# Four-layer image kernel: y of two directions in one accumulator, the next direction's operands made one image early, and a free order of the units

## What is computed

```python
def step(h, inp):
    dt_t, B_t, C_t, u_t = inp
    dA = jnp.exp(dt_t[..., None] * A)
    h = dA * h + (dt_t * u_t)[..., None] * B_t[:, None, :]
    y = jnp.einsum('bdn,bn->bd', h, C_t)
    return (h, y)
...
y = ys.transpose(1, 0, 2) + uc * Dp
y = y * jax.nn.silu(z)
return jnp.einsum('bld,od->blo', y, out_proj_w)
```

## Time and profile before

| | us |
|---|---|
| median of three executions | 13798.05 |
| the profiled execution | 13793.3 |
| its span, first to last instruction | 13791.5 |
| PE busy | 12088.6 (88%) |
| DVE busy | 12598.5 (91%) |
| ACT busy | 12052.7 (87%) |
| POOL busy | 12608.1 (91%) |

### The profile page before, as it was taken

The page is one execution under the profiler, slowest core; times in us unless marked ns, Lnnn a source line. Parts: engine busy times, 40 slices in busy tenths (PEclk is TensorE's granted clock), DMA queues, the critical chain, the costliest instruction groups (busy, mean ns, idle before and its releaser), DMA issues.

```text
span 13791.5 us, 184501 instructions
## 1 busy us (share of the span) xinstructions
PE 12088.6 (88%) x68188; PEld 8349.2 (61%) x68188; DVE 12598.5 (91%) x8502; ACT 12052.7 (87%) x18757; POOL 12608.1 (91%) x3786
## 2 busy tenths in 40 slices
PE   7888889898888888888888888888888888888886
PEld 4566666666666666666666666666666666666654
DVE  7999999999999999999999999999999999999985
ACT  6889888889888898888898888888888988889875
POOL 6999999999999999999999999999999999999985
PEclk8999999999999999999999999999999999999987
DMA  5555555555555555555555555555555555555552
GB/s 188 217 222 218 220 213 223 224 213 221 221 217 219 219 217 222 218 219 221 215 222 217 221 220 220 218 216 222 218 223 215 219 217 218 224 215 222 217 200 110
DMA packets 517060, 2965.20 MB, mean 215 GB/s; under 512 B 57818, under 2 KB 57914, under 8 KB 253890
## 3 DMA queue, kind: packets, MB, share of 16 engines
q1 hardware_dynamic: 516162, 2953.40, 56.8%
HBM read 2889.73 MB, written 46.66 MB: 213 GB/s over the span
## 4 chain that ended last, share of the span: by engine, by line
POOL 27%; issue 25%; DVE 18%; ACT 16%; PE 12%; DMA 0%; POOLq 0%; DVEq 0%; SPq 0%; ACTq 0%
POOL ring L983 18%; DVE ring L1469 10%; POOL ring L966 8%; DVE slot L1455 6%; PE work L1481 5%; PE y_acc L1496 4%; ACT L1000 4%; ACT ring L1160 3%; ACT z_t L1069 2%; PE slot L1496 2%; ACT slot L1160 2%; PE y_acc L1481 1%; ACT work L1052 1%; ACT stack L1050 1%; DVE du L1282 1%
## 5 line engine op out<-in xcount | busy, mean ns | idle before, releaser
L983 POOL TENSOR_TENSOR ring<-ring,c_rows 128x2048 f32<-128x2048 f32 x2048 | 9295.3, 4546 | 814.1 <-DVE ring L1469 809.7
L1469 DVE TENSOR_TENSOR_SCAN ring<-ring,slot 128x1024 f32<-128x1024 f32 x2752 | 6251.9, 2281 | 161.9 <-ACT ring L1160 66.4
L1496 PE MATMUL y_acc<-wk,ring 128*128 128x128 f32 x32768 | 4506.5, 285 | 625.6 <-POOL ring L983 592.6
L1496 PEld LDWEIGHTS y_acc<-wk,ring 128*128 128x128 f32 x32768 | 3975.3, 147 | 1431.0 <-POOL ring L983 766.2
L966 POOL TENSOR_TENSOR ring<-du,b_rows 128x1024 f32<-128x1024 f32 x1344 | 3182.1, 2369 | 180.9 <-PE y_acc L1496 77.4
L1469 DVE TENSOR_TENSOR_SCAN ring<-slot,ring 128x1024 f32<-128x1024 f32 x1344 | 3058.3, 2276 | 277.3 <-POOL ring L966 244.6
L1160 ACT ACTIVATE ring<-dt,a_neg 128x1024 f32<-128x1024 f32 x2752 | 3069.7, 1140 | 52.0 <-PE y_acc L1496 42.2
L1455 DVE TENSOR_TENSOR slot<-du,slot 128x1024 f32<-128x1024 f32 x1952 | 2361.8, 1210 | 53.1 <-PE slot L1481 50.0
L1000 ACT ACT_TABLE_LOAD x1825 | 2341.5, 1283 | 32.0
L1069 ACT ACTIVATE z_t<-du_t,b_t 128x128 f32<-128x128 f32 x6400 | 2037.1, 391 | 40.1 <-PE slot L1496 17.5
L1481 PE MATMUL work<-h_new,fused 128*128 128x512 f32 x4096 | 1914.3, 601 | 46.1 <-ACT b_t L1072 30.6
(11 more groups left out here) (178 smaller groups left out, 9800.0 us busy)
## 6 DMA issues: line engine op xcount, KB each, us to landing
c_rows<-cb_rows_scratch SPq DMA_DIRECT2D x2048, 1024.0 KB, 4.6
b_rows<-cb_rows_scratch SPq DMA_DIRECT2D x1344, 512.0 KB, 5.5
x_next<-in_x SPq DMA_DIRECT2D x32, 512.0 KB, 5.6
x_new_scratch<-x_next SPq DMA_DIRECT2D x32, 512.0 KB, 6.7
h_old<-h_new SPq DMA_DIRECT2D x32, 512.0 KB, 3.2
x_old<-x_new_scratch SPq DMA_DIRECT2D x32, 512.0 KB, 7.3
out<-x_old SPq DMA_DIRECT2D x32, 512.0 KB, 3.2
cb_rows_scratch<-stack SPq DMA_DIRECT2D x128, 100.0 KB
```

Of the source, the lines that this page charges most:

```text
L983: pool.tensor_tensor(pair, pair, c_rows[:, k % CB_BUFS, :, :], ALU.mult).then_inc(prod_ready, 1)
L1469: dve.tensor_tensor_scan(slot, a, b, 0.0, MUL, ADD).then_inc(scan_done, 1)
L1496: ins = pe.matmul(chunk(out_t, j), chunk(x, j), kc("ident"), is_transpose=True, start=start and j % (BANK // P) == 0, stop=stop, skip_grou ...
```

## The change

**Order of the units.** `pass_of` and `parts_of` put the half outside and the direction inside within each pair of directions. The passes of an image run (d, h) = (0,0), (1,0), (0,1), (1,1), (2,0), (3,0), (2,1), (3,1).

**Accumulator.** `y_acc` is started with every 32nd unit. Two passes, the two directions of a pair on one half, go into it. The takes on ACT (L1076) and the addition of `yz` in PE (n = 5) are gone. DVE takes after passes 1, 3, 5 and 7, as many as before.

**Operands.** Those of direction 1 (convolution, projection, `cb_rows`) and the first z gate are made in the image in front, behind those of direction 0. For image 0, `begin_plan` makes them. `stack` and `b_t` get a third buffer. SP stores direction 1's rows at the start of an image, and stores those of 2 and 3 ahead of passes 4 and 5.

**Free order.** The units of an engine are lines of their own for the planner: on DVE the D inputs and the scans, on POOL the P inputs and the products, on PE the spreads or turns and the sums. They are laid beside the side steps by due time and readiness. `SHIFTS` has new values, now for units too.

**Kinds.** `KINDS` is new: 53 D, 49 P and 26 Z for an image. By pass, in the new order, P has 6, 6, 7, 6, 7, 6, 5 and 6 (before: 5, 6, 4, 7, 8, 3, 3 and 5).

```diff
-KINDS = ('DPDPDDDDDPZPDPDZ', 'DPDZDPDZDPZPDPDP', 'DDDDDPZPDZDPZDDP', 'DPDPDPZZZPZPDPDP',
-         'DPZPDPZPDPPDZPDP', 'DPDPDPDDDDZZDPDZ', 'DPDPDPDDZZDDDZDZ', 'DPDPDPDDDDZDZPZP')
+KINDS = ('DPPZZDDDZPZPPPDZ', 'DDDDDPZPDPZPPDDP', 'DPDZPDDZPPZPDDPP', 'DZPDDZPZPPZZDPDP',
+         'DPZPPDPZDPPDZDPD', 'DPDPDZPZPDPDDZDP', 'DDPDDPPPDDZDZDPD', 'DPDDZDDDPPDPZPPZ')
...
+    return {"D": [[("b", u) for u in of("D")], [("scan", u) for u in range(UNITS)]],
+            "G": [[("input", u) for u in of("P")], [("prod", u) for u in range(1, UNITS, 2)]],
+            "P": [[("zturn" if kind_of(u) == "Z" else "spread", u) for u in turned], [("sum", u) for u in range(UNITS)]],
+            "A": [[("decay", u) for u in range(UNITS)]]}
...
+        ops += held_back(conv_after(0, 0), ("h1", 1)) + conv_after(1, 0) + conv_after(0, 1) + project_after(0, over(3))
+        ops += gate_z(0, 0, [("take", 5)]) + conv_after(1, 1)
+        ops += rows_after(project_after(1, over(6)), 1, ("scan", UNITS - 5))
...
+    o = held_back(o, ("fuse", 1, TAPS - 1)) + gate_z(0, 0) + conv(1, 0) + conv(1, 1)
+    o += project(1)
...
+                store_rows(1, base, ("A", 0))
...
-                    if n == 5 and d % 2:
-                        halves(y_acc, kc("ident"), yz[:, d // 2, h, :], False, False)
                     pe.wait_ge(prod_ready, s * PAIRS + u // 2 + 1)
-                    turn(y_acc, ring[:, u % RING, :], n == 0, n == NST - 1).then_inc(sum_done, 1)
+                    turn(y_acc, ring[:, u % RING, :], u % (2 * NST) == 0, (u + 1) % (2 * NST) == 0).then_inc(sum_done, 1)
```

More of the change, by code:

```diff
@@ L144, in silu_pair, with conv, gate_z, project @@
     return steps + [step(("silu", of, d, h, c), "A", key(c)) for c in range(2)]
-def operands(d, first=False):
-    steps = []
[L150 to L155, removed]
+def conv(d, h):
+    return silu_pair("u", d, h, "conv_in", [(k,) for k in range(TAPS)])
+def gate_z(f, h, after=()):
+    return silu_pair("z", f, h, "z", [()], after)
+def project(d):
+    steps = []
     for c in range(2):
@@ L456, in wanted @@
             by[("zmul", u, 1)] = u - 1.5
-    by[("take", "before")] = 4
-    for p in range(PASSES - 1):
+    for p in range(1, PASSES - 1, 2):
         by[("take", p)] = p * NST + NST + 4
-    by[("turned_y", "this", 1, 0, 1)] = UNITS - 4
+    by[("silu", "z", 0, 0, 1)], by[("silu", "z", 1, 1, 1)] = UNITS + 2 * NST, UNITS
     want = deadlines(streams, by, pace)
@@ L602, in image_streams @@
     takes = []
-    for p in range(PASSES - 1):
-        f, t, h = p // 4, p // 2 % 2, p % 2
-        after = [("sum", p * NST + NST - 1)]
-        if t == 0 and not first:
-            after += [(("post", 1) if h else ("angles",)) if f else ("mix", 4, 1)]
-        takes += [step(("take", p), "D" if t else "A", None, after)]
-        if t:
-            takes += turn_y("this", f, h)
+    for p in range(1, PASSES - 1, 2):
+        f, h = p // 4, p // 2 % 2
+        after = [("sum", p * NST + NST - 1)] + ([("silu", "z", f, h, 1)] if p > 1 else [])
+        if not first:
+            after += [("angles",) if f else ("mix", 4, 1)]
+        takes += [step(("take", p), "D", None, after)] + turn_y("this", f, h)
     zs = []
@@ L635, in count @@
     def count(steps, e):
-        return sum(x[2] == e for x in steps)
+        return sum(x[1] == e and x[3] is not None for x in steps)
     def bases(kind, s):
@@ L647, in numbers @@
         n, out = dict.fromkeys("PADG", 0), {}
-        for x in steps:
-            n[x[2]] += 1
-            out[x[1]] = (x[2], n[x[2]])
+        for name, e, _, after in steps:
+            if after is not None:
+                n[e] += 1
+                out[name] = (e, n[e])
         return out
@@ L654, in four_layers, with order_of, image_of @@
     plan_n = {kind: numbers(plan) for kind, plan in plans.items()}
-    def at_place(plan, e):
-        out = {}
-        for x in plan:
-            if x[2] == e:
-                out.setdefault(x[0], []).append(x)
-        return out
+    def order_of(plan, e):
+        return [x for x in plan if x[1] == e]
+    def image_of(name, s):
+        k = name[0]
+        if name in front_names or k in ("cb_rows", "part", "rest", "xproj", "turn_b", "turned_b", "conv_in") and name[1] < 2:
+            return s + 1
+        if k == "silu" and name[1] == "u" and name[2] < 2:
+            return s + 1
+        if (k[:3] == "dt_" or k in ("turn_du", "turned_du")) and name[1:3] == (0, 0):
+            return s + 1
+        return s
+    front_names = {x[0] for x in front()}
     with ExitStack() as ctx:
@@ L943, in step @@
                 ins.then_inc(side["G"], 1)
-            for _, name, e, _, after in before:
+            for name, e, _, after in before:
                 if e == "G":
@@ L950, in image @@
             def image(kind, s):
[L951 to L956 removed]
+                base, of = bases(kind, s), plan_n[kind]
                 def make_input(u):
@@ L983, in image @@
                     pool.tensor_tensor(pair, pair, c_rows[:, k % CB_BUFS, :, :], ALU.mult).then_inc(prod_ready, 1)
-                side_steps(END["G"])
+                for name, _, _, after in order_of(plans[kind], "G"):
+                    if name[0] == "input":
+                        make_input(name[1])
+                    elif name[0] == "prod":
+                        times_c(name[1])
+                    else:
+                        hold(pool, "G", base, of, after)
+                        step(name, s)
             each_image(pool, image)
-            for _, name, e, _, after in finish:
+            for name, e, _, after in finish:
                 if e == "G":
@@ L1123, in step @@
                 ins.then_inc(side["A"], 1)
-            for _, name, e, bank, after in before:
+            for name, e, bank, after in before:
                 if e == "A":
@@ L1469, in image @@
                     dve.tensor_tensor_scan(slot, a, b, 0.0, MUL, ADD).then_inc(scan_done, 1)
-                side_steps(END["D"])
+                for name, _, bank, after in order_of(plans[kind], "D"):
+                    if name[0] == "b":
+                        times_b(name[1])
+                    elif name[0] == "scan":
+                        scan(name[1])
+                    else:
+                        hold(dve, "D", base, of, after)
+                        step(name, image_of(name, s), bank_of[bank])
             each_image(dve, image)
-            for _, name, e, bank, after in finish:
+            for name, e, bank, after in finish:
                 if e == "D":
```

365 lines of the change are left out of this document (171 added, 194 removed), and 98 rows, old and new, of the table SHIFTS.

## The result

The changed kernel takes 14372.49 us (median of four, 14369.08 to 14382.40), the kernel before 13797.58 in the same comparison. The ratio is 1.0418, 95% interval 1.0400 to 1.0436: 575 us slower, where 168 us faster was forecast. The profiled execution spans 14367.3 us.

A forecast was written before the change was run, and what follows sets the result against it. DVE was taken to bound some passes and POOL others. Start 130.4, first image 420, thirty middle images 12486, last 450 and finish 138.4 sum to 13624.8, with profile and median offsets 13630 us; range 13440 to 13890.

The forecast's parts named there:

- The store of rows: Direction 1's operands, made one image early: ACT's `cb_rows` should find SP's store done, since it is issued in 0.27 us.
- POOL's waits for scans: Middle images: POOL's 24.0 us an image of waiting for DVE's scans go nearly all.
- the idle term: POOL's idle time in a middle image: 6 us, bounds 0 and 28.5, giving 416.2 us an image.
- its line between faster and slower: POOL's idle time per middle image from which the idle-time rival decides: 11.6 us.
- a balance of loads by pass: All eight passes now ask more of POOL than of DVE, so POOL's waits for scans go nearly all.
- The turn of the image: Between images, direction 1's early operands on ACT: 2 us taken; as slower rival 8 us a turn, 13880 us, chance 0.14.
- POOL's and DVE's work: Middle image, from the new kinds: POOL busy 410.2 us instead of 393.9, DVE 382.8 instead of 392.7.
- The takes: Four ACT copies an image go, 4.1 us of ACT; fewer handovers worth 0 to 2.5 us, counted within the idle time.
- The start: Ahead of the first product: direction 1's operands and z gate add 29 us, between 20 and 40.
- DMA: 7 more B rows of 512 KB, 4% more at a share of 58%, cost nothing.
- POOL's idle time stays: Slower rival: the 28.5 us an image are what engines in fixed order lose to each other; 14350 us, chance 0.11.
- POOL idle over 12 us with DVE full in the same pass: Sign, per image, that would make the forecast wrong.

The follow-up runs named there:

- e1_rows32: The changed kernel with all 32 rows of B and C stored instead of 31; 13969.49 us, ratio 1.0125 to the kernel before.
- e16_pool_load_moved: The kernel before plus four unused POOL products an image at units 91, 93, 97 and 109, away from `group_rstd`; 13854.49 us, ratio 1.0042.
- e14_pool_load: The kernel before plus four unused POOL products an image at units 87, 89, 103 and 107; 14155.19 us, ratio 1.0258.
- e15_act_tie: The kernel before with ACT's decays of units 87, 89, 103 and 107 held for the scan two units back; 13976.34 us, ratio 1.0134.
- e3_in_order: The changed kernel, 31 rows, with each engine's units in the old fixed order and side steps laid anew; 15017.89 us, ratio 1.0885.
- e8_before_no_copy: The kernel before without ACT's four takes an image, PE's waits for them and PE's additions of `yz`; 13818.52 us, ratio 1.0016.
- e17_before_46p_moved: The kernel before with four D units made P at units 92, 94, 98 and 108, away from `group_rstd`; 14248.52 us, ratio 1.0327.

## Why the prediction was wrong, point by point

**The store of rows** is the step that failed first, and the larger part: 13.5 of the 24.4 us by which a middle image missed (440.6 against 416.2). I wrote that such a store is issued in 0.27 us and that ACT "should find the store done". The row prices the issue; what waits is the landing. SP waited 9.7 us a store for it. The row to read stood beside it in the same timeline: the next load 3.0 us after the store, for a store of 25 rows. And the store is not the same after the change, since a line outside the diff derives its row count from `KINDS`. I priced the B rows that are read back and never asked what the new table does to the store.

**POOL's waits for scans** are nearly all of the rest. "The 24.0 us an image that POOL waits for scans go nearly all" was the step on which the forecast rested. With the store mended, 375.8 / 30 = 12.5 us of them stay. The other two waits, put at 4.1 us, measured (70.3 + 65.0) / 30 = 4.5. So the idle term is 17.3 us instead of 6, and the 11.3 us more, with POOL's busy time 0.4 under the forecast, are the rest of the miss. The forecast's own arithmetic holds with it: its line between faster and slower stood at 11.6 us, and 30 x (17.3 - 11.6) = 171 us over 13798 gives 13969, against 13969.5 measured for `e1_rows32`.

The reason I gave was a balance of loads by pass. The traces say where it held. Cut at the first product of each pass, mean of the thirty middle images, POOL's idle time is 4.6, 0.0, 3.9, 5.7, 0.0, 4.2, 3.8 and 6.3 us in the passes 0 to 7 before, and 1.5, 0.0, 0.9, 6.8, 1.7, 0.0, 1.9 and 4.5 in `e1_rows32`. In six passes together it fell from 16.5 us to 6.0, as I had reckoned for all eight. In passes 3 and 7 it stayed: 12.0 before, 11.3 after. There no engine is busy for more than 93% of the pass in either kernel, so a better balance had little to give; the earlier trace rows showed this of pass 3 already. It is also not true that all eight passes now ask more of POOL than of DVE: pass 3 has one P unit less than before, and DVE is busy 57.2 us in it, POOL 56.9. In image 9, pass 7 before; then passes 3 and 7 of `e1_rows32`, and POOL's longest stop in pass 3:

```profile
4267.15:4321.81 54.66, 47.03 (x257) 32.83 (x255) 46.48 (x28) 46.84 (x76) 47.69 (x14) 0.91 0.57 217
```

```profile
4139.62:4203.17 63.55, 53.02 (x285) 34.36 (x285) 57.13 (x44) 58.87 (x104) 56.92 (x21) 0.97 0.52 195
4353.29:4409.81 56.52, 44.25 (x276) 31.63 (x277) 45.96 (x27) 51.27 (x73) 52.30 (x17) 0.97 0.65 246
...
4162.72 4.55 POOL L1049 TENSOR_TENSOR ring<-ring,c_rows 128x2048 f32<-128x2048 f32 x1 [6.15 <-DVE ring L1526]
```

That one stop, in front of the product of units 52 and 53, is 6.2 us in the mean image, half of the 12.5; DVE has layer 2's side steps between the scans there. Whether the six passes gained by the kinds or by the new order was not taken apart. `e16_pool_load_moved` shows that idle time can take load, 7.7 us of 9.5; `e14_pool_load` and `e15_act_tie` show what the balance leaves out, waits that one engine passes on to another. Which ties hold the rest in the new plan is not settled. The waits that grew most are DVE's for slots from PE (50.0 us before, 529.7 after, 363.6 in `e1_rows32`) and ACT's for slots from DVE (270.8, 591.4, 583.3); no run took one of them away alone.

**The turn of the image** was put at 2 us with 8 as its bound. ACT waited 4.5 us there, but for the store (1.3 for PE), and that wait is gone with 32 rows. There POOL idles 2.6 us in front of an image's first product, 2.5 before. As a rival (13880) it did not happen.

**POOL's and DVE's work** came as forecast: POOL 409.8 us an image (410.2), DVE 11513.9 / 30 = 383.8 (382.8). **ACT** has 381.2 instead of 375.4. The new plan changes its function tables more often: 1941 loads at 1.28 us against 1825 before is 116 more, 4.7 us an image. I had no term for it. The free order is not the main reason: `e3_in_order` has 1910.

**The takes** and the handovers were worth nothing (`e8_before_no_copy`, 24 us slower), just under the low end of what I gave them. **The start** grew by 34.9 us (29 forecast, 20 to 40), 3.4 of it the slow store: 132.9 us with 32 rows, thus 31.5. **The first image** took 430.1 us (420) and the last 442.6 (450), both inside their bounds. **DMA:** "nothing" held for the bytes, at a share of 0.59 against 0.58, and was wrong for the queue behind the store.

**The rivals.** "POOL's idle time stays" gave 14350, and 14372 was measured: the idle time is 30.7 us an image against 28.5. That the two numbers meet is luck. Its mechanism (engines in fixed order lose to each other what a pass has to spare) can account for 17.3 us at most; the other 13.5 are the store, which it did not have. The rule of the Trainium skill that I set beside it, "Perfetto Trace Analysis", "Identifying the Most-Contended Engine", gave the right sign here. By `e16_pool_load_moved`, work on that engine is still not dear as such. What I named as a sign that the forecast fails, POOL idle over 12 us with DVE full in the same pass, did not come that way: in the one pass where DVE idles under 2 us, pass 6, POOL idles 1.0. Pass 3 loses the most. The kernel after, that pass in image 9:

```profile
4251.17:4320.90 69.73, 54.89 (x286) 35.94 (x285) 57.57 (x44) 58.67 (x104) 56.83 (x22) 0.93 0.49 179
```

POOL 56.8, DVE 57.6 and ACT 58.7 of 69.7 us: this is a pass that waits, not one that is out of balance. The stop of 6.39 us behind the store lies in it; without it, in `e1_rows32`, the pass takes 63.6 us with nobody full.

## What to carry to other kernels

Price a transfer that somebody waits for by its landing, read from the start of what is held behind it, and recompute its shape when the change alters a table from which the shape is derived. Idle time on a top engine is not simply room: before you fill it, look which small steps of that engine others wait for, and what else the moved work ties together. Split the idle time by stretch before you spend it. Where a pass shows no engine full, a better balance of work had little to give here.

## What the runs showed of the hardware

Of five row counts for the same store in the kernel before, SP's waits for it were 2.1 us (25 rows), 1.9 (28, `e17_before_46p_moved`), 6.8 (29), 7.2 (31) and 2.0 (32). While such a store of 31 rows was alone on its way, the DMA share was 0.06 at 24 GB/s; loads just before it ran at 0.94 and 377 GB/s. One useless row made the wait over three times shorter (7.2 to 2.0 us), and the kernel after 403 us faster. In the kernel after the wait also holds what SP had issued just before: 9.7 us with 31 rows, 4.3 with 32. Of the 10.8 us between the store at 4285.11 and the next load, 5.2 passed before its first packet, and its 31 packets took 4.8.
